# First attention of a four-layer kernel: probabilities times tokens in three passes of rounded parts

## The reference, cut to what matters

```
kv = concatenate([memory, layer_input])                 # 128 tokens x 128
q, k, v, r = layer_input @ Wq, kv @ Wk, kv @ Wv, pe @ Wr
scores = (einsum(q + content_bias, k) + rel_shift(einsum(q + position_bias, r))) / sqrt(64)
scores = where(mask, -1e9, scores)
attn = softmax(scores)
out = layer_norm(layer_input + (attn @ v, heads side by side) @ Wo)
```

## Time and profile before

| | us |
|---|---|
| Median of 3 runs | 1923.54 (1917.91 to 1925.33) |
| The profiled execution, its own time | 1926.87 |
| Its span | 1925.3 |
| TensorE matmul busy | 1615.0 (84% of the span) |
| VectorE busy | 1327.5 (69%) |
| ScalarE busy | 1195.7 (62%) |
| GpSimd busy | 947.5 (49%) |

### The profile page before, as it was taken

One profiled execution on the slowest core, in us unless ns is written; L12 is line 12 of the kernel. 1 busy time (PEld: TensorE's weight loads), 2 busy tenths in 40 slices (PEclk: granted clock), 3 DMA queues, 4 the chain that ended last, 5 costly groups with the idle time before them and its releaser, 6 DMA issues. The chain is left out here.

```text
span 1925.3 us, 54847 instructions
## 1 busy us (share of the span) xinstructions
PE 1615.0 (84%) x17114; PEld 1295.0 (67%) x17114; DVE 1327.5 (69%) x4084; ACT 1195.7 (62%) x3451; POOL 947.5 (49%) x1389
## 2 busy tenths in 40 slices
PE   6999999999997869999999776379999994448982
PEld 6788888888885747667777662157777774336761
DVE  3777777778776638888877536668888883346872
ACT  2776776776774327677887335468888871137771
POOL 2454454354441454556665434535454444636773
PEclk8999999999999879999999797679999995569996
DMA  8866666666662022221000000000000000136765
GB/s 230 158 146 153 147 149 145 151 152 137 156 149 72 1 85 104 103 96 52 21 18 13 1 0 1 0 4 1 0 10 14 12 9 27 46 122 200 217 210 158
DMA packets 214819, 167.06 MB, mean 87 GB/s; under 512 B 27632, under 2 KB 188784, under 8 KB 214448
## 3 DMA queue, kind: packets, MB, share of 16 engines
q1 hardware_dynamic: 206128, 142.75, 29.8%
q0 software_dynamic: 8576, 22.88, 3.6%
HBM read 91.79 MB, written 73.76 MB: 86 GB/s over the span
## 5 line engine op out<-in xcount | busy, mean ns | idle before, releaser
L738 ACT ACTIVATE sb_probs<-sb_probs,sb_work 128x128 f32<-128x128 f32 x512 | 198.6, 405 | 117.5 <-DVE sb_work L641 117.5
L281 POOL TENSOR_SCALAR sb_next_var_eps<-sb_next_moments 128x1 f32<-128x1 f32 (+1 forms) x184 | 45.4, 247 | 430.1 <-DVE sb_next_moments L721 241.3
L890 POOL TENSOR_TENSOR sb_work<-sb_work,sb_cols 128x512 f32<-128x512 f32 x128 | 134.2, 1048 | 193.5 <-ACT sb_work L1111 122.7
L1035 DVE TENSOR_REDUCE sb_work<-PS 128x8 f32<-128x512 f32 x256 | 175.3, 685 | 39.8 <-PE PS L932 38.1
L1037 DVE TENSOR_TENSOR sb_work<-PS,sb_work 128x512 f32<-128x512 f32 x256 | 177.1, 692 | 8.8
L1069 ACT ACTIVATE sb_work<-sb_work 128x512 f32<-128x512 f32 x256 | 161.6, 631 | 32.3 <-DVE sb_work L1037 26.4
L906 PE MATMUL PS<-sb_ident,sb_work 128*128 128x128 f32 x1024 | 151.5, 286 | 16.4 <-ACT sb_work L1111 9.7
L959 PEld LDWEIGHTS PS<-sb_v_ones,sb_work 128*64 128x64 f32 x4096 | 132.9, 140 | 23.6 <-issue 15.2
L959 PE MATMUL PS<-sb_v_ones,sb_work 128*64 128x18 f32 x4096 | 145.0, 214 | 4.0 <-ACT sb_work L1075 2.8
L1075 ACT ACTIVATE sb_work<-PS 128x512 f32<-128x512 f32 x256 | 139.4, 595 | 9.6 <-PE PS L906 6.4
L906 PEld LDWEIGHTS PS<-sb_ident,sb_work 128*128 128x128 f32 x1024 | 111.6, 143 | 47.5 <-issue 32.0
(11 more groups left out here) (281 smaller groups left out, 4470.4 us busy)
## 6 DMA issues: line engine op xcount, KB each, us to landing
rel_scratch<-sb_work SPq DMA_DIRECT2D x64, 516.0 KB, 7.7
sb_work<-rel_scratch SPq DMA_DIRECT2D x64, 512.0 KB, 6.6
expert_rows<-sb_blank SPq DMA_DIRECT2D x36, 520.0 KB, 2.9
sb_w_up<-expert_halves SPq DMA_DIRECT2D x23, 512.0 KB, 3.6
sb_w_down<-expert_halves SPq DMA_DIRECT2D x23, 512.0 KB, 3.4
expert_halves<-sb_e_halves POOLq DMA_DIRECT2D x16, 512.0 KB, 6.2
sb_work<-expert_rows SPq DMA_DIRECT2D x23, 260.0 KB, 3.3
sb_e_raw<-e_W POOLq DMA_DIRECT2D x16, 256.0 KB, 5.7
```

Of the source, the lines that this page charges most:

```text
L738: ins = e.activation(probs[:, j], probs[:, j], ACT.Exp, bias=neg_max[:, j:j + 1], scale=-1.0, accum_out=row_sum[:, j:j + 1])
L890: e.tensor_tensor(k_masked[:, u3], k_sb[:, u3].rearrange("p (b k) -> p b k", b=2).unsqueeze(2) .to_broadcast([P, 2, 4, S]), col("place").u ...
L1035: e.tensor_reduce(top, mine, AX.X, ALU.max).then_inc(sem("att_max_ready"), 1)
```

## The change

- The tokens of a tile are split into a rounded high part `kv_hi` and a low part `kv_lo` on GpSimd, at the end of its step and for the next tile (two new instructions of 128x256, with three waits, counted by a new semaphore `l0_kv_split`).
- The transposed probabilities are split too: ScalarE writes the rounded high part `probsT_hi` (two new instructions of 128x1024, ahead of the exponentials of group 0), and VectorE writes the low part `probsT_lo` by a subtraction in place of its two copies.
- TensorE's four products of full fp32 type become four `product_in_parts`, twelve passes of 512 columns of type fp32r.
- VectorE takes the tokens' parts of tile n+3 (L673 to L679) ahead of `add_relative(0)` and `(1)`; before they stood after these two.
- TensorE leaves out waits that others imply: those of queries, keys and kept relative scores ahead of the content scores, those of the tokens' parts and of `l0_q_kept` and `l0_pkvT_kept` in the keys' stage; of the four waits for `l0_rows_done` in the relative stage one for all four stays.
- At the start, one loaded weight lies in another place of the work buffer, and two semaphores are merged into others.

```
-            VO, rel_bias, w_q0, w_k0_hi, w_k0_lo, rT, probs, probsT, pkvT = (
+            VO, rel_bias, w_q0, w_k0_hi, w_k0_lo, probs, probsT_hi, probsT_lo, pkvT = (
...
# GpSimd, end of step n
+                if has(1):
+                    t, v = n + 1, (u + 1) % 2
+                    wait_alone(e, sem("l0_kv_loaded"), 48 * 4 if isinstance(t, int) and t < 4 else 48 * t + 48)
+                    wait_alone(e, sem("l0_pkv_done"), 4 * (t - 2) + 4)
+                    e.tensor_tensor(kv_hi[:, v], kv_in[:, (u + 1) % 4],
+                                    zeros[:, 0:1].unsqueeze(2).to_broadcast([P, 2, D]), ALU.add)\
+                        .then_inc(sem("l0_kv_split"), 1)
+                    wait_alone(e, sem("l0_kv_split"), 2 * t + 1)
+                    e.tensor_tensor(kv_lo[:, v], kv_in[:, (u + 1) % 4], kv_hi[:, v].bitcast(F32), ALU.subtract)\
+                        .then_inc(sem("l0_kv_split"), 1)
...
# TensorE, content scores
-                    e.wait_ge(sem("l0_q_kept"), 2 * t + 2)
-                    wait_alone(e, sem("l0_k_kept"), 4 * t + 4)
+                    passed = has(0) and has(2)
+                    if not passed:
+                        e.wait_ge(sem("l0_q_kept"), 2 * t + 2)
+                        wait_alone(e, sem("l0_k_kept"), 4 * t + 4)
...
-                            if i == 0:
+                            if i == 0 and not passed:
...
# TensorE, probabilities times tokens
-                        e.wait_ge(sem("l0_probsT_kept"), 2 * n + (1 if j == 0 else 2))
+                        if j == 1 or j == 0 and not has(3):
+                            e.wait_ge(sem("l0_probsT_kept"), 2 * n + j + 1)
+                        if j == 0:
+                            e.wait_ge(sem("l0_kv_split"), 2 * n + 2)
                         if j == 3 and has(3):
                             e.wait_ge(sem("l0_kv_kept"), 2 * (n + 3) + 2)
-                        e.matmul(PS[:, (j + 1) % 4], kv_in[:, u, b], probsT[:, 8 * G:8 * G + 8, S * b:S * b + S],
-                                 start=True, stop=True).then_inc(sem("l0_pkv_done"), 1)
+                        heads, queries = slice(8 * G, 8 * G + 8), slice(S * b, S * b + S)
+                        product_in_parts(e, PS[:, (j + 1) % 4], (kv_hi[:, u % 2, b], kv_lo[:, u % 2, b]),
+                                         (probsT_hi[:, heads, queries], probsT_lo[:, heads, queries]))\
+                            .then_inc(sem("l0_pkv_done"), 1)
...
# TensorE, relative scores and keys
-                    e.wait_ge(sem("l0_kv_kept"), 2 * t + 1)
+                    if not has(0):
+                        e.wait_ge(sem("l0_kv_kept"), 2 * t + 1)
...
-                                        e.wait_ge(sem("l0_rows_done"), 4 * (n + 1) + g + 1)
+                                        if g == 0:
+                                            e.wait_ge(sem("l0_rows_done"), 4 * (n + 1) + 4)
...
# VectorE
                 if has(0):
                     for half in range(2):
-                        e.wait_ge(sem("l0_probsT_done"), 4 * n + 2 * half + 2)
-                        e.tensor_copy(probsT[:, 8 * half:8 * half + 8].rearrange("p (g i) k -> p g (i k)", g=2),
-                                      PS[:, 2 * half:2 * half + 2]).then_inc(sem("l0_probsT_kept"), 1)
-                if has(1):
-                    e.wait_ge(sem("l0_rel_read"), 32 * (n + 1) + 32)
-                    add_relative(0)
-                    add_relative(1)
+                        e.wait_ge(sem("l0_probsT_rounded"), 2 * n + half + 1)
+                        r = slice(8 * half, 8 * half + 8)
+                        e.tensor_tensor(probsT_lo[:, r].rearrange("p (g i) k -> p g (i k)", g=2),
+                                        PS[:, 2 * half:2 * half + 2],
+                                        probsT_hi[:, r].bitcast(F32).rearrange("p (g i) k -> p g (i k)", g=2),
+                                        ALU.subtract).then_inc(sem("l0_probsT_kept"), 1)
                 if has(3):
                     ... the tokens' parts of tile n+3, as before
                 if has(1):
+                    e.wait_ge(sem("l0_rel_read"), 32 * (n + 1) + 32)
+                    add_relative(0)
+                    add_relative(1)
                     add_relative(2)
                     add_relative(3)
                     normalise(0)
...
# ScalarE
+                if has(0):
+                    for half in range(2):
+                        e.wait_ge(sem("l0_probsT_done"), 4 * n + 2 * half + 2)
+                        e.activation(probsT_hi[:, 8 * half:8 * half + 8].rearrange("p (g i) k -> p g (i k)", g=2),
+                                     PS[:, 2 * half:2 * half + 2], ACT.Copy).then_inc(sem("l0_probsT_rounded"), 1)
                 if has(1):
                     exponentials(0)
```

## The result

The changed kernel takes 1963.51 us (median of 6 runs, 1960.09 to 1966.97) against 1921.67 us of the kernel before on the same chips (6 runs, 1917.91 to 1927.69). The ratio is 1.0214 with a 95% interval of 1.0199 to 1.0229: slower by 41.8 us. The forecast was 1958, slower by 34.3.

The account below looks back on a forecast made before the run. TensorE's own instructions were taken to bound the stage, with 1.0 us of slack before the queries. Steps +32.8, start -1 and tail +2.5 made +34.3 on 1923.54, so 1957.8, say 1958 us; range 1938 to 1980.

Parts of the forecast that it names:

- The path and its places: Transposes, ScalarE's rounding, VectorE's low and tokens' parts, add_relative(0), exponentials, first product copy: queries start 1.23 us later.
- The saving of the passes: TensorE's products in twelve passes: 0.67 us a step less work, all lost in idle time before the queries.
- No hold between GpSimd and VectorE: VectorE's new subtraction, with one PSUM input, is not held up by GpSimd; otherwise some 25 us in all.
- The steady step: Each of steps 0 to 28 grows by 1.13 us, between +0.6 and +1.6; +32.8 us in all.
- The 0.1 taken off for the waits left out: Two places behind the queries where TensorE drops implied waits: 0.1 us a step saved, between 0 and 0.3.
- The start: Step -1, where TensorE idled 5.08 us for the tokens' high part: freed early by the new order, -1 us.
- The tail: Steps 29 to 31: two steps pay 1.11 us each and the last a few tenths, +2.5 us.
- the term that the prediction took at nothing "with that cover": GpSimd's split of the tokens, covered by the queries' wait: nothing; without that cover up to 0.3 us a step.
- ScalarE just in time: ScalarE is free at about T+17.0 (T: step's first transposes), first keys there at T+17.1: no term.
- The rival with ScalarE as the bound: ScalarE binds, or GpSimd holds the subtraction: a step +1.6 to +2.1 us, 1972 to 1986 us; chance 0.13.
- the chance of 0.04 for the clock: Rival: new idle time lowers TensorE's clock, queries at half rate cost 1.83 us a step, 2011 us; chance 0.04.

Follow-up runs that it names:

- tokens_after_groups: Changed kernel with VectorE's tokens' parts back behind add_relative(0) and (1): 1943.68 us, ratio 1.0111 to the kernel before.
- tokens_between_groups: Changed kernel with VectorE's tokens' parts between add_relative(0) and add_relative(1): 1928.12 us, ratio 1.0027 to the kernel before.
- copies_first: Changed kernel with ScalarE's four product copies ahead of the exponentials of group 0: 1909.65 us, ratio 0.9929 to the kernel before.
- before_tokens_ahead: Kernel before with one edit, VectorE's tokens' parts ahead of add_relative(0): 1955.37 us, ratio 1.0168.
- before_waits_out: Kernel before with only TensorE's implied waits left out, as in the change: 1920.38 us, ratio 0.9988.
- one_pass: Changed kernel with only the first (high times high) of each product's three passes: 2007.65 us, ratio 1.0435 to the kernel before.
- one_pass_copies_first: Changed kernel with one pass of three per product and ScalarE's product copies ahead of group 0's exponentials: 1882.76 us, ratio 0.9792 to the kernel before.
- copies_first_again: Repeat of copies_first, beside a variant with that order only in full steps: 1908.64 us, ratio 0.9931 to the kernel before.
- before_copies_first: Kernel before, full fp32 products kept, with ScalarE's four product copies ahead of the exponentials of group 0: 1928.87 us, ratio 1.0027.

## Why the prediction was right, and where its sizes were off

**The path and its places: right.** All six times of the path came within 0.07 us. That is not luck, since the terms that they are added up from came out one by one. The rounding copy, which no row had in its size, was put at 1.03 and takes 1.02; the subtraction was put at 1.22 and takes 2.36 for the pair as the copies did; the tokens' parts take 1.06. GpSimd's split was put at T+3.6 and ends at T+3.57 (348.64 to 352.21), as its timeline in the same step shows:

```profile
350.73 0.60 POOL L450 TENSOR_TENSOR sb_kv_hi<-sb_kv_in,sb_zeros 128x256 fp32r<-128x256 f32 x1
...
351.48 0.73 POOL L454 TENSOR_TENSOR sb_kv_lo<-sb_kv_in,sb_kv_hi 128x256 fp32r<-128x256 f32 x1
```

The experiments that take one link out of the path or shift it (tokens_after_groups, tokens_between_groups, copies_first, before_tokens_ahead) moved the step to 18.50, 18.04, 17.21 and 18.98 against 18.4, 18.1, 17.2 and 18.9 to 19.0 expected.

**The saving of the passes: right that it is lost.** It is 0.65 a step (17.86 against 17.21) once nothing else binds, against 0.67 from the earlier trace rows. In the changed step, too, passes follow each other at 0.23 us (352.90 to 355.22, ten distances). The Trainium skill's page "TensorE: Matmul & The Clock Gate" (section "Back-to-back issue gap") gives about 131 ns for 512 columns; no trace here agrees with that.

**No hold between GpSimd and VectorE: as counted.** The low part kept its 2.36 for two while GpSimd's split ran beside it. The page "SBUF — State Buffer" of the Trainium skill (section "Who interferes with whom") has it that a VectorE instruction with at most one SBUF input does not contend with GpSimd; this trace agrees.

**The steady step: 1.25, not 1.13.** Two terms were missing or wrong. The 0.1 taken off for the waits left out is not there: before_waits_out keeps its step, and the distance from transposes to scores is 1.84 in both traces (329.89 to 331.73 in the earlier trace rows, 348.64 to 350.48 after). And the queries take 1.88 in place of 1.79, all of it at the first of the sixteen, which comes out of the wait: it takes 0.38 us for 0.27, and the second starts 0.21 behind it, where all others, also that of the second half, follow at 0.11, as before the change. The prediction had these 0.09 nowhere. Together 0.19, less 0.07 for a path slightly shorter than reckoned, make 0.12 a step, 36.1-32.8 = 3.3 us in all.

**The start: +0.1, not -1.** TensorE's queries of step -1 do come earlier, and so do its relative scores behind them, at 54.80 for 56.62. But they come behind a new wait and at half rate, with a granted clock of 0.50 (0.94 before), and the first steady step starts at 62.04 against 61.96.

```profile
54.80 3.79 PE L595 MATMUL PS<-sb_rT,sb_work 64*128 64x128 f32 x32 [4.80 <-ACT sb_work L788]
```

Between the traces of the kernel before and its three variants this start varies by 1.9 us (61.13 to 62.99), so the term was too small to be tested.

**The tail: +4.4, not +2.5.** The two tail steps cost 26.32 against 24.74, +1.6 where 2.2 was put. The last is the mis-sized one: 15.06 us from its transposes to the end of the stage against 12.29, +2.8 where a few tenths were put. This is the table of stretches at its passes, first after, then before (fp32 products):

```profile
648.40:653.70 5.30, 5.27 (x13) 4.16 (x14) 0.37 (x1) 1.79 (x3) 0.47 (x1) 0.50 0.24 99
```

```profile
609.20:613.00 3.80, 3.78 (x8) 1.36 (x8) 1.09 (x1) 1.79 (x3) 0.57 (x1) 1.00 0.34 138
```

and the waits ahead of it after the change:

```profile
645.39 1.06 PE L511 MATMUL PS<-sb_ident,sb_probs 128*128 128x128 f32 x8 [1.90 <-DVE sb_probs L670]
...
648.43 0.77 PE L1230 MATMUL PS<-sb_probsT_hi,sb_kv_hi 128*128 128x512 f32 x1 [1.98 <-POOL sb_kv_lo L454]
...
653.26 0.59 PE L1230 MATMUL PS<-sb_probsT_hi,sb_kv_lo 128*128 128x512 f32 x1
```

Two stretches of idle time, 1.90 and 1.98 us, lie 1.1 us of work apart; the second ends on GpSimd's split, which in full steps is hidden and here is not, as its start waits for VectorE's statistics. This is the term that the prediction took at nothing "with that cover". From the second eight transposes to the first pass there are 3.04 us (645.39 to 648.43) against 1.51 to the first product before (607.71 to 609.22), +1.5. The passes then start 0.427 apart in place of 0.230, at a granted clock of 0.50: 12 x 0.20 = 2.4 us. Less the 1.0 that the passes save at the full clock, this is the +1.4 between 5.25 us for them and 3.81 for the four products before. The prediction had neither. The first passes of the last step are as slow, 0.76 to 0.77 us for 0.47, in all six traces that have the split and all three passes.

**ScalarE just in time: it had more room.** It waited 0.52 us for the first keys, as its timeline in the changed kernel shows, where the sum said none, since its four copies ran without a wait (2.02 us) where before the last waited for its product.

```profile
365.80 0.60 ACT L798 ACTIVATE sb_work<-PS 128x512 f32<-128x512 f32 x1 [0.52 <-PE PS L1230]
```

The rival with ScalarE as the bound never came near.

**The sum.** 3.3 in the steps, 1.1 at the start and 1.9 in the tail make 6.3 us more than forecast; behind the stage the changed kernel's trace is 0.6 shorter, and 5.7 is what the forecast of 1957.8 lacks of the median, 1963.51. That the time still came within 0.3% rests on the steady step, which was understood. Of the chance of 0.04 for the clock one can't say the same: the wait came out at 1.63 us where 2.02 by the same measure was the longest that the prediction knew to be harmless, and the last section shows that 2.02 is not always harmless.

## What to carry to other kernels

Where one engine runs without a gap, read the slack of every chain that comes back to it, from its own start to the copy that it waits for, before adding an instruction to that chain or putting one ahead in it: here the slack was 1.0 us and the additions 2.2. An in-order engine's queue makes dependences that the data don't have; the whole loss, and the gain that the change was good for, hung on one order (exponentials ahead of copies that don't need them), and moving it in the full steps turned +2.1% into -0.8%. Less work for an engine that waits can make it slower, where the wait that takes the work's place brings its clock down. An order that is right in the full steps can be wrong in the tail, where another wait is last.

## What the runs showed of the hardware that was not expected

Less work can make TensorE slower through its clock. In steady steps the traces are clear: one stretch of 1.6 us of idle time a step left the granted clock at 1.00 over all 29 steps of the changed kernel (the queries that follow it take 1.88 us); 2.50 us, with 0.32 a little before, brought a stretch of half rate in each of the 29 steps of one_pass. The stage lost 43 us by it, and nothing once the wait was gone (one_pass_copies_first).

Waits near 2 us are not so clear. In the tail of the kernel before, eight transposes behind a wait of 2.02 us took 1.06, at a granted clock of 1.00. In before_waits_out the same eight, behind the same wait and the same work, ran at half rate; behind the next such wait the transposes were fast, and the products after them at a granted clock of 0.67:

```profile
593.33 1.94 PE L499 MATMUL PS<-sb_ident,sb_probs 128*128 128x128 f32 x8 [2.02 <-DVE sb_probs L652]
608.42 1.06 PE L499 MATMUL PS<-sb_ident,sb_probs 128*128 128x128 f32 x8 [2.02 <-DVE sb_probs L652]
609.93 5.40 PE L539 MATMUL PS<-sb_probsT,sb_kv_in 128*128 128x512 f32 x8 [0.44 <-DVE sb_probsT L665]
```

Another wait shortly ahead goes with a fall more often, but doesn't decide it. In copies_first_again the 2.02 came behind a wait of 1.53, with eight transposes between them, and the rate was halved, in both steps of the tail and in both traces of this kernel; behind 1.69, in before_copies_first, it fell both times as well, once a group later. Behind 1.30, in one_pass_copies_first, it stayed at 1.00 both times.

```profile
571.93 1.06 PE L511 MATMUL PS<-sb_ident,sb_probs 128*128 128x128 f32 x8 [1.53 <-DVE sb_probs L670]
575.02 1.94 PE L511 MATMUL PS<-sb_ident,sb_probs 128*128 128x128 f32 x8 [2.02 <-DVE sb_probs L670]
```

And two kernels that do the same work in the tail differ: behind waits of 1.6 and then 1.98 us, the granted clock was 1.00 in the changed kernel (first row) and 0.62 in tokens_after_groups (second).

```profile
631.30 1.06 PE L511 MATMUL PS<-sb_ident,sb_probs 128*128 128x128 f32 x8 [1.98 <-DVE sb_probs L670]
611.83 1.23 PE L511 MATMUL PS<-sb_ident,sb_probs 128*128 128x128 f32 x8 [1.98 <-DVE sb_probs L670]
```

So neither the length of a wait near 2 us nor the waits before it settle in these traces whether the clock falls; what decides it stays open. One execution that kept its clock through such a wait is no proof that the next one will, and a change that adds a wait of this size should be priced both ways.
